# A macaron block on one core: roots in two parts, four banks for turned rows, items 4 and 5 joined, first projection in the first program

## The reference

```
x = x + 0.5 * ffn(layernorm(x))
x = x + mamba(layernorm(x))
x = x + 0.5 * ffn(layernorm(x))

ffn(x):   x = fwht(x * SU_ug) / 64
          h = silu(x @ W_gate.T * s) * (x @ W_up.T * s')       (2048 wide)
          return (fwht(h * SU_dp) / 64) @ W_down.T * s''
mamba(x): gate, xBC, dt = split(x @ in_proj.T)                 (1024, 1280, 64)
          xBC = silu(causal conv of 4 taps); x, B, C = split(xBC)
          dt = clip(softplus(dt + dt_bias)); A = -exp(A_log)
          chunks of 64 tokens, 64 heads of 16, state 128:
            within a chunk  y = (C B^T * exp(segsum(A dt))) x dt
            between chunks  states decay, y += C states * exp(cumsum)
          y = (y + D x) * silu(gate); y = rmsnorm(y) * norm_w
          return y @ out_proj.T
```

## Time and profile before

| | |
|---|---|
| three runs | 1681.34 us median (1678.62 to 1681.82) |
| profiled execution | 1676.78 us |
| its span | 1674.8 us, mean granted clock of TensorE 0.996 |
| TensorE matmul busy | 1629.1 us (97%) |
| VectorE / ScalarE / GpSimd busy | 61% / 38% / 23% |
| DMA | 290.46 MB, 173 GB/s, 16 engines 52.8% busy |

### The profile page before, as it was taken

The page is one execution under the profiler, slowest core; times in us unless marked ns, Lnnn a source line. Parts: engine busy times, 40 slices in busy tenths (PEclk is TensorE's granted clock), DMA queues, the critical chain, the costliest instruction groups (busy, mean ns, idle before and its releaser), DMA issues.

```text
span 1674.8 us, 25013 instructions
## 1 busy us (share of the span) xinstructions
PE 1629.1 (97%) x9672; PEld 1314.6 (78%) x9672; DVE 1018.4 (61%) x2022; ACT 630.1 (38%) x936; POOL 377.2 (23%) x298
## 2 busy tenths in 40 slices
PE   6999999989999999999999999999999999999998
PEld 3777777867888778888877888877888887887886
DVE  6543345766676776767776777777776664443333
ACT  4333333454433464333454334355333342112111
POOL 1656653012221212222122122222122230000000
PEclk9999999999999999999999999999999999999999
DMA  9755554655445454454435445445454447566563
GB/s 312 277 188 217 198 189 163 214 190 165 155 156 163 130 165 153 159 165 149 153 128 175 157 149 170 155 135 183 153 167 154 154 126 226 163 191 184 180 203 121
DMA packets 253427, 290.46 MB, mean 173 GB/s; under 512 B 14464, under 2 KB 211200, under 8 KB 244096
## 3 DMA queue, kind: packets, MB, share of 16 engines
q1 hardware_dynamic: 253312, 288.88, 52.8%
HBM read 238.51 MB, written 50.33 MB: 172 GB/s over the span
## 4 chain that ended last, share of the span: by engine, by line
PE 63%; DVE 11%; ACT 3%; issue 2%; POOL 0%; DVEq 0%; ACTq 0%; POOLq 0%
PE bank L1120 25%; PE bank L1161 14%; PE bank L1083 10%; PE bank L1177 4%; PE bank L1246 2%; DVE m_cv L1703 2%; PE bank L1233 2%; PE bank L1195 2%; DVE m_sta L1747 1%; PE bank L1217 1%; DVE m_sta L1749 1%; DVE xn L1676 1%; PE bank L1205 1%; DVE m_mv L164 1%; ACT m_hb L1462 1%
## 5 line engine op out<-in xcount | busy, mean ns | idle before, releaser
L1120 PE MATMUL bank<-fxT,wj 128*128 128x512 f32 x1992 | 471.3, 391 | 2.3 <-DVE fxT L1669 1.5
L1120 PEld LDWEIGHTS bank<-fxT,wj 128*128 128x128 f32 x1992 | 373.8, 188 | 81.0 <-DVE res L1688 3.1
L1161 PE MATMUL bank<-m_wd,m_hb 128*128 128x512 f32 x1152 | 287.4, 395 | 6.8 <-DVE m_hb L1682 6.3
L1161 PEld LDWEIGHTS bank<-m_wd,m_hb 128*128 128x128 f32 x1152 | 213.9, 189 | 54.2 <-issue 11.9
L1083 PE MATMUL bank<-xT,wi 128*128 128x512 f32 x912 | 227.1, 398 | 4.7 <-PEq L191 2.6
L1462 ACT CAST m_hb<-xn 128x512 fp32r<-128x512 f32 x96 | 59.5, 620 | 449.6 <-DVE xn L1676 449.6
L1083 PEld LDWEIGHTS bank<-xT,wi 128*128 128x128 f32 x912 | 169.1, 189 | 42.9 <-issue 7.2
L1688 DVE TENSOR_TENSOR res<-bank,res 128x512 f32<-128x512 f32 x192 | 132.6, 691 | 91.0 <-PE bank L1161 90.0
L2001 POOL TENSOR_TENSOR m_L<-m_L,m_GT 128x512 f32<-128x512 f32 x36 | 52.8, 1468 | 459.0 <-ACT m_L L1471 459.0
L1676 DVE SCALAR_TENSOR_TENSOR xn<-bank,sc,xn 128x512 f32<-128x512 f32 x96 | 71.8, 748 | 130.5 <-PE bank L1120 130.4
L1456 ACT ACTIVATE xn<-bank,sc 128x512 f32<-128x512 f32 x96 | 66.0, 687 | 143.1 <-PE bank L1120 137.9
(11 more groups left out here) (211 smaller groups left out, 2151.0 us busy)
## 6 DMA issues: line engine op xcount, KB each, us to landing
wj<-ug_split SPq DMA_DIRECT2D x167, 512.0 KB, 4.3
m_wd<-dn_split SPq DMA_DIRECT2D x48, 1024.0 KB, 4.8
wi<-in_split SPq DMA_DIRECT2D x76, 512.0 KB, 3.3
ug_split<-b_wu SPq DMA_DIRECT2D x8, 2048.0 KB, 14.3
m_wo<-out_split SPq DMA_DIRECT2D x32, 512.0 KB, 4.1
wi<-ug_split SPq DMA_DIRECT2D x25, 512.0 KB, 4.3
in_split<-b_msp SPq DMA_DIRECT2D x20, 512.0 KB, 3.8
raw<-in_wug SPq DMA_DIRECT2D x8, 1024.0 KB, 6.9
```

Of the source, the lines that this page charges most:

```text
L1120: ins = pe.matmul(to[:], w[:, a, k, :], fxT[:, b, k, :], start=(k == 0 and i == 0), stop=(k == KH - 1 and i == 2))
L1161: ins = pe.matmul(F[t % 2][:], hb[:, a, j, ck(t)], wd[:, b, j, :], start=(j == 0 and n == 0), stop=(j == 1 and n == 2))
```

## The change

Eight edits, all of them of order, of banks or of waits; no instruction of the computation is added.

1. `roots` yields in the middle of `rsqrt`, after two of the four Newton rounds. At b = 4 (`other`) and b = 6 (`following`) the first part is stepped ahead of `states`, and the second where all of it stood. In item 4 both parts stay where they were.
2. `beside_turn` has four banks: S[0], S[1], A (Y for item 5), X. Turns 2 and 3 no longer wait for turns 0 and 1 to be read; `products`, `ends_out` wait for turns instead.
3. In `mixer`'s first unit ScalarE does `gate`, `x_silu`, `end_decays` in this order; TensorE and VectorE are reordered there too.
4. In b = 0 of items 1 to 3 both halves of `in_proj(q, 5)` come before `new_states`, and `up0` goes last. SP loads the weights of `in_proj(q + 1, 5)` before `keep` and `heads`.
5. Items 4 and 5 are one loop: the rows of item 5 are written at b = 5 of item 4 into `L`, turned at b = 6 into `xT`, and VectorE writes their low part at b = 7. `gate0(40)` is then issued as in any unit.
6. `down_last`: the last unit's `down` goes over j outermost into four banks.
7. `in_proj(0, 0)` becomes `project_ahead`, at the end of the first program.
8. In the first program's last unit `high_blocks` and `low_blocks` go forward.

```diff
 def rsqrt(eng, ch, y, v, t, scale=1.0):
...
-    for _ in range(4):
+    for i in range(4):
+        if i == 2:
+            yield
...
+            def project_ahead():
+
+                pe.wait_ge(s_tl, turns["x", 3, TPG - 1] + 1)
+                pe.wait_ge(s_wi[0], 16)
+                for k in range(KH):
+                    for i, (a, b) in enumerate(PASSES):
+                        ins = pe.matmul(U[0][:], wi[0][:, a, k, :], xT[0][:, b, k, :], start=(k == 0 and i == 0), stop=(k == KH - 1 and i == 2))
+                ins.then_inc(s_in, 1)
...
                 down(UNITS - 1, (t, t + 1))
+            project_ahead()
...
             silu(UNITS - 1, 1)
+            high_blocks(UNITS - 1)
             rows(3, (0, 1))
...
             hidden(n, 0)
+            low_blocks(n)
             hidden(n, 1)
...
+        def beside_bank(i, t):
+
+            return (S[0], S[1], A if i <= BATCH else Y, X)[t]
...
                 if more:
                     load_in(m0 + 2 * NB + 4)
+                    load_in(m0 + 2 * NB + 5)
                     keep(q + 1)
                     heads(q + 1, 0)
-                    load_in(m0 + 2 * NB + 5)
                     load_in(m0 + 2 * NB + 6)
...
                 elif t == 0:
-                    pe.wait_ge(s_z, NB * min(i, BATCH))
-                    wait(pe, s_v, i - 1 if i > BATCH else 0)
-                    wait(pe, s_fxlo, TPG * (i - 1) - 1)
+                    pe.wait_ge(s_z, NB * mixed)
+                elif t == 1:
+                    pe.wait_ge(s_st, NB * mixed)
+                elif t == 2:
+                    pe.wait_ge(s_L, QUADS * NB * mixed)
                 else:
-                    pe.wait_ge(s_st, NB * min(i, BATCH))
-                    wait(pe, s_fxlo, TPG * (i - 1))
+                    pe.wait_ge(s_ex, NB * mixed)
...
+            def down_last(at):
+
+                pe.wait_ge(s_wd, 16 * (at + 1))
+                for j in range(2):
+                    pe.wait_ge(s_hi, 2 * at + j + 1)
+                    pe.wait_ge(s_lo, 2 * at + j + 1)
+                    for t in range(TPG):
+                        for n, (a, b) in enumerate(PASSES):
+                            ins = pe.matmul(end_bank(t)[:], hb[:, a, j, ck(t)], wd[:, b, j, :], start=(j == 0 and n == 0), stop=(j == 1 and n == 2))
+                        if j:
+                            ins.then_inc(s_d, 1)
...
-                wait(pe, s_ex, NB * q)
+                wait(pe, s_fxlo, TPG * q)
...
-            in_proj(0, 0)
             in_proj(0, 1)
...
-                    if b == 0:
-                        if q:
-                            up0(at)
+                    if at == 0:
+                        in_proj(q, 5, 0)
                         decay(q, b, 1)
+                        decay(q, b, 2)
+                        in_proj(q, 5, 1)
+                        decay(q, b, 3)
+                        new_states(q, b)
+                    elif b == 0:
                         in_proj(q, 5, 0)
+                        decay(q, b, 1)
+                        in_proj(q, 5, 1)
                         decay(q, b, 2)
                         new_states(q, b)
-                        in_proj(q, 5, 1)
                         decay(q, b, 3)
+                        up0(at)
...
                     ydiag(q, b)
+                    if at == 0:
+                        up1(at)
                     from_states(q, b)
...
+            for at in range(NC * BATCH, NC * ITEMS):
+                q, b = at // NC, at % NC
+                pair = last_pair(q, b)
+                if not opens(at):
+                    down(at - 1, 0, last_pair(q, b - 1) + 1 if b else 0)
+                    down(at - 1, 1)
                     if q == BATCH and b == 1:
                         sums(q - 1)
...
+                up0(at)
+                gate1(at)
+                if q == BATCH and b == 6:
                     for t in range(TPG):
-                        down(at, t)
+                        beside_turn(q + 1, t)
+                up1(at)
...
+                if at < NC * ITEMS - 1:
+                    gate0(at + 1, pair + 1)
+            down_last(NC * ITEMS - 1)
...
+            gate(0, 0)
+            x_silu(0, 0)
             end_decays(0)
-            x_silu(0, 0)
-            gate(0, 0)
...
+                        if at == 0 and j == 2:
+                            hidden_high(at, 0)
...
+                if q == BATCH and b == 5:
+                    for t in range(TPG):
+                        beside_row(q + 1, t)
+                hidden_high(at, 1)
+                if at < NC * ITEMS - 1:
                     silu(at + 1, 0)
+                if q == BATCH and b == 6:
+                    for t in range(TPG):
+                        beside_turn(q + 1, t)
...
+                    if b == 4:
+                        next(other)
+                    if b == 6 and more:
+                        next(following)
+                    if at == 0:
+                        hidden(at, 0)
+                        hidden_low(at, 0)
                     states(q, b)
...
+                if q == BATCH and b == NB - 1:
+                    for t in range(TPG):
                         beside_turn(q + 1, t)
+                hidden(at, 0)
+                hidden_low(at, 0)
```

More of the change, by code:

```diff
@@ L144, in normalize @@
     yield
-    roots(dve, st, mv, ch)
+    yield from roots(dve, st, mv, ch)
     yield
@@ L670, in _ @@
             hidden_high(UNITS - 1, 1)
[L671 to L675, removed]
+            for t in range(TPG):
+                turn(("x", 3, t))
         @block.vector
@@ L765, in _ @@
                     own.done(dve.bn_stats(st[:, t, :], res[:, t, :]))
-            roots(dve, st, mv, own)
+            run(roots(dve, st, mv, own))
             bias(0, 2 * TPG)
@@ L813, in _ @@
                     next(third)
+                    next(third)
                     bias(TPG, TPG)
@@ L1119, in half_up @@
                     for i, (a, b) in enumerate(PASSES):
-                        ins = pe.matmul(to[:], w[:, a, k, :], fxT[:, b, k, :], start=(k == 0 and i == 0), stop=(k == KH - 1 and i == 2))
+                        ins = pe.matmul(to[:], w[:, a, k, :], frm[:, b, k, :], start=(k == 0 and i == 0), stop=(k == KH - 1 and i == 2))
                 return ins
@@ L1946, in _ @@
                     keep_rows(q + 1)
-            for q in range(BATCH, ITEMS):
-                other = stats(beside(q + 1), 1) if q < ITEMS - 1 else None
-                for b in range(NB):
-                    at = NC * q + b
-                    pair = last_pair(q, b)
-                    if b:
-                        add_down(at - 1, 0)
-                        add_down(at - 1, 1)
+            other = stats(beside(ITEMS - 1), 1)
+            for at in range(NC * BATCH, NC * ITEMS):
+                q, b = at // NC, at % NC
+                pair = last_pair(q, b)
+                if not opens(at):
+                    add_down(at - 1, 0)
+                    add_down(at - 1, 1)
@@ L1968, in _ @@
[L1968 to L1980 removed]
+                    add_down(at - 1, 2)
@@ new lines, in _ @@
+                    add_down(at - 1, 3)
+                if q == BATCH and b == NB - 1:
+                    for t in range(TPG):
+                        beside_turn(q + 1, t)
+                hidden(at, 0)
+                hidden_low(at, 0)
+                if q == BATCH and b == 1:
+                    norm(q - 1)
+                if q == BATCH and b == 2:
+                    ending(q - 1)
+                if q == BATCH and b in (3, 4):
+                    next(other)
+                if q == BATCH and b == 4:
+                    next(other)
+                    bias(1, s_fs)
@@ L1982, in _ @@
+                hidden(at, 1)
+                if pair >= 0:
+                    add_out(pair, 0)
+                hidden_low(at, 1)
+                if pair >= 0:
+                    for t in range(1, TPG):
+                        add_out(pair, t)
+            for t in range(TPG):
+                add_down(NC * ITEMS - 1, t)
         @block.gpsimd
```

165 lines of the change are left out of this document (65 added, 100 removed).

## The result

The changed kernel takes 1660.36 us, median of four runs (1659.12 to 1660.81), against 1679.98 for the kernel before on the same chip (four runs, 1676.52 to 1681.82). The ratio is 0.9884, 95% interval 0.9866 to 0.9903: 1.2% faster. The forecast was 1663.8, its range 1658 to 1671.

What follows compares the result with a forecast made beforehand. TensorE's matmuls were taken to bound the kernel, busy 1629.1 of 1674.8 us. Terms 5.9 + 2.6 + 1.6 + 2.1 + 2.3 + 3.0 = 17.5 us, off the 1681.3 median, gave 1663.8, range 1658 to 1671.

Steps and rivals of the forecast that it cites:

- Joint of items 4 and 5: Between item 4's last `up1` and item 5's first `gate0`: waits and half-rate go, 5.9 us gained, bounds 4.5 and 6.0.
- Last unit: Final `down` over four banks runs during the 2.49 us wait for the second hidden half: 2.3 us gained, bounds 1.6 and 2.6.
- Start: Start of the second program: shorter softplus chain and two table loads saved on ScalarE, 3.0 us gained, bounds 1.8 and 4.5.
- that is 2.2 for TensorE: Second program's start: everything 0.55 us later but 2.73 us of matmuls done, 2.2 for TensorE, though the softplus chain bounds.
- Four banks: Ends of items 0 to 2: turn 2 no longer waits for VectorE to read turn 0, 2.6 us gained, bounds 1.3 and 2.65.
- Next `down(., 2)` needs `add_down(., 0)`... The new wait is `products`: Ends of items 0 to 2: `add_down` is through before; `products` waits on turn 3, ready about 1 us before `in_proj(q + 1, 3)` ends.
- Order of b = 0: Items 1 to 3: the 0.52 us wait of `in_proj(q, 6)` for `conv` goes three times, 1.6 us gained, bounds 0.8 and 1.6.
- Roots: Two parts at b = 4 and b = 6: the next unit's `down` waits less, 2.1 us gained, bounds -1.0 and 3.4.
- Net 0.3 for each, 2.1 for seven: Roots in seven units: `hidden(., 1)` gains 0.4 us, the in-projection loses 0.15, net 0.3 each, 2.1 in all.
- The first rival: Waits come back at neighbours in the hand-written orders: 12 us gained in all, 1669 us, chance 0.17.
- its roots term: Waits come back, at the split roots: they bring 0 us.
- Slower by the part caught at every step: VectorE ahead of `states`, seven units: eleven steps held 0.93 us each, 6.4 us lost per unit, 45 in all, 1711; chance 0.03.

Runs made afterwards that it cites:

- both mends: Changed kernel with roots split at b = 4 alone and the kept state's transfers ahead of the weight load: median 1659.32 us, ratio to before 0.9887.
- the ends back: Changed kernel with items 4 and 5 and the last unit as before the change: span 11.6 us above the changed kernel's 1658.4.
- roots over two units: Changed kernel with b = 4's roots split late over b = 4 and b = 5, b = 6's whole and late: span 0.7 us below 1658.4.

## Why the prediction held, and which steps failed

The forecast was right: the sum of the parts is 17.5 and the profiles differ by 16.4. That it came so near owes something to errors of both signs.

- *Joint of items 4 and 5*: 5.9 predicted, 5.89 found, 5.87 on undoing it. What was priced at nothing (rows ahead of `hidden_high(37, 1)`, low parts at b = 7) cost nothing.
- *Last unit*: 2.3, found 2.7. The output tiles' queueing was no 0.3: four adds end at 1655.91, the span at 1658.4, 2.5 later, as before (1672.36 and 1674.8).
- *Start*: 3.0, found 3.25, 3.5 by the mean of nine starts. The start of before is known from one execution, and those nine differ by 1.45, so the distance from 3.0 is no finding. The first decay exp came at 366.97 where 367.0 was forecast, and the weights in time. Counted from the `down`s the gain is 0.9 at the first exp of the softplus chain (forecast 0.34), 1.05 at the first products, 2.4 at the first decay exp, 3.25 at unit 1; between the products and the decay exp it is the table loads, 1.3 by undoing them. The barrier opened 0.5 later, as forecast (0.55). What failed is what the projection was put forward for, "that is 2.2 for TensorE": with it back the barrier opens at once, 1.06 instead of 2.61 behind the `down`s, by the blocks made earlier alone, and the softplus chain's first exp comes 0.8 sooner. The projection in the first program brings nothing on top. The last 0.9, behind the decay exp, I haven't taken apart; neither the reordering of TensorE and VectorE there nor the blocks' move was undone by itself.
- *Four banks*: 2.6, found 2.0. The step "Next `down(., 2)` needs `add_down(., 0)`... The new wait is `products`" looked at TensorE's neighbours in VectorE; in item 3 the state's transfer ended last.
- *Order of b = 0*: 1.6, and with four banks 4.2 against 3.77, which leaves 1.7 for the order by subtraction; no run undid TensorE's order alone. The load ahead of `keep` was priced at nothing in both directions. It is worth 2.5, for the new order stands on it, and it slows the state by over 1 us, which decides in item 3. The text followed SP's queue for the up weights and not for the state, which is stored, waited for and loaded back on the same queue.
- *Roots*: 2.1, found 1.1. The failed step is "Net 0.3 for each, 2.1 for seven": it took b = 6 to be like b = 4. At b = 4 the net is 0.45, at b = 6 the early part loses 0.28 and the freed `down` gains nothing, since TensorE then waits for ScalarE's exp and for `xT` in b = 7. The first rival said so ("ScalarE's rows in b = 7, whose exp is not set by the part that moved") and was given 0.17 as a whole; its roots term was near the truth for b = 6 alone.
- *Slower by the part caught at every step*: two steps were held, not eleven.

The medians differ by 19.6, more than the 16.4 of the profiles. The profiled execution of before was among its fastest (1676.78 where the runs reached 1681.82), and the changed kernel's runs spread 1.7 us where those of before spread 5.3. The spread alone proves little: the four runs with both mends spread 5.2. Over the changed kernel and its runs the first program put all that follows up to 3 us earlier or later, and may do so before. The run with the ends back shows another source: a wait that in one execution costs 2.5 costs 4.1 in another, when the clock falls behind it. Whether either holds for the median of before is not shown; I didn't profile its slower executions.

## What to carry to other kernels

Line up equal instructions of two traces and read the gain place by place: here the spans of single runs were 1 to 3 us apart for reasons that lie ahead of every edit. A wait is worth its length only where nothing else is due at the same point: 0.46 at b = 6 and 0.88 in item 3 were worth nothing. When work is moved earlier, move its load, and then see which small transfer with a longer way (store, wait, load back) that load now meets.

## What I had not expected of the hardware

The start of the second program, the same instructions each time, took 50.91 to 52.36 us, and the windows show where TensorE ran at half rate: only between 374 and 378 us (clock 0.60) in the shortest, from 366 to 374 (0.50) in the two longest. In the changed kernel it fell twice, at 362 and again at 376, each time behind waits of 1.84 and 1.59 us. The same two waits stand in the run with roots over two units, and the clock fell behind neither (1.00 at 362 and at 376). After the same wait of 2.49 us in the last unit it fell in one execution and not in another. So the length of a wait doesn't tell by itself whether the clock falls behind it, and the clock of one profile is not that of the next: a reading of the start needs several executions.
